# Quantised adapter FFN: h and g transposed as pairs of bytes, scale rows through DRAM, new orders on every engine

## The chip, the cores and the metric

One core of a Trainium2 chip runs the kernel. The metric is device time in microseconds (us). The kernel before has a median of 359.89 us over 3 runs, from 357.31 to 361.01.

## The reference

For each of the 8 batches b, x[b] is 256 tokens by 1024 features, in float32.

- The adapter product: y = x[b] @ W[ids[b]]^T, where W has 16 adapters of 1024x1024 and ids picks one for each batch.
- The FFN on y: a layer norm with gamma and beta gives h. Then two "dynamic quant" linears with an exact GELU between them:

```
s  = max(|row|) / 127                  (one scale for each row, of activations and of weights)
q  = clip(round(row / s), -127, 127)   (whole numbers from -127 to 127)
f1 = (q_h @ q_w1^T) * s_h * s_w1 + b1
g  = gelu(f1)
f2 = (q_g @ q_w3^T) * s_g * s_w3 + b3
out = x + f2
```

## The kernel before

**Tiling.** A batch has two token tiles t of 128 rows. PSUM holds a_ps (two banks, the adapter product), f_ps (two banks, everything of the FFN) and t_ps (four banks, transposed adapter weights).

**The adapter product** is made exact enough by splitting x and W into a high and a low part in a rounded float32 format: three matmuls hi*hi, hi*lo, lo*hi (L1114 to L1116, `products`). A batch has four units u, each of two pieces k. One piece is 12 matmuls of 128x512 on PE (`piece`, L1119). W comes from DRAM in units of 1 MB into the two buffers of w_nat. DVE transposes it in 32x32 blocks into t_ps (`transpose_w`), ACT rounds the high part (`split_w`), DVE subtracts to get the low part (`low_w`). x goes the same way, its low part on POOL (`low_x`).

**The FFN of batch f** runs inside the turn p = f + 1 of a loop over batches. The stages for each token tile:

1. ACT normalises y, POOL multiplies by gamma and adds beta (`scale_and_shift`), DVE takes the row maximum and the scale (`scales_h`), and ACT scales and rounds (`round_h`, by adding the constant 1.5*2^23, so that the whole number stands in the low 16 bits of the float32 word).
2. PE transposes those 16-bit halves (`transpose_h`, `transpose_tile` L1141), eight 128x128 blocks a tile, the tiles into one bank of f_ps each. ACT copies them as int16 to bf16 (`take_h`).
3. PE multiplies by w_q[0] (`ffn1`, 16 matmuls of 128x512 a tile), DVE rescales (`rescale1` L901), POOL adds b1, ACT does GELU, DVE takes the maximum (`scales_g`), ACT rounds (`round_g`).
4. The same again for g: `transpose_g`, `take_g`, `ffn2`, then `scale_ffn2` on ACT, and on POOL the weight scales, the residual and b3 (`finish`, `residual`).

**The head** treats batches 0 and 1: their x and W are transposed on PE (`transpose_first`, 20 steps in FIRST), and the 16 row tiles of w1 and w3 are scaled, rounded, transposed and taken (`max_prep`, `round_prep`, `prepare`, `take_prep`). The two rows of weight scales are made on PE and ACT:

```
for i in range(RT):
    column = wq_scale[:, RT * n + i:RT * n + i + 1].broadcast_to([P, P])
    dst = f_ps[:, i // RB, (i % RB) * P:(i % RB + 1) * P]
    last = pe.transpose(dst, column, ident[:])
```

**The loop** is turns p = 2 to 6. **The tail** (`last_period` on PE, ACT and DVE) finishes batch 7 and the FFNs of batches 6 and 7, with a_ps and t_ps as further banks for the FFN.

**What sets the order.** Each engine has its own in-order list, written out by hand; semaphores tie them. All loads and stores are issued from the SP queue, also in order: a wait of one blocks all behind it. PE's order of a turn before:

```
piece(p, 2, 0)   transpose_h(p - 1, 0), (p - 1, 1)   piece(p, 2, 1)   ffn1(p - 1, 0)
piece(p, 3, 0)   piece(p, 3, 1)                      ffn1(p - 1, 1)
piece(p + 1, 0, 0)  transpose_g(p - 1, 0)            piece(p + 1, 0, 1)  ffn2(p - 1, 0)
piece(p + 1, 1, 0)  transpose_g(p - 1, 1)            piece(p + 1, 1, 1)  ffn2(p - 1, 1)
```

## Time and profile before

| | |
|---|---|
| median of 3 runs | 359.89 us |
| the profiled execution | 362.2 us, span 360.4 us, granted clock 0.99 |
| PE busy | 338.1 us (94%) |
| DVE busy | 282.6 us (78%) |
| POOL busy | 264.3 us (73%) |
| ACT busy | 226.4 us (63%) |
| DMA | 67.35 MB, 70.2% of 16 engines' span |

PE is the matmul side of TensorE, PEld its weight loads. A matmul's duration in the rows contains the overlap with its neighbours: the distance of one start to the next tells what one costs. "Idle before" names who released an engine that stood still. The span runs from the first to the last instruction of the core.

### The profile page before, as it was taken

What the parts mean: (1) busy time and instruction counts of PE and PEld (TensorE: products, weight loads), DVE (VectorE), ACT (ScalarE), POOL (GpSimd) and SP (SyncE); (2) the same over time, 40 slices, a digit from 0 to 9 for tenths busy, and PEclk for the clock granted to TensorE, in tenths of its full rate; (3) what the DMA queues carried; (4) which work ended last, traced back from release to release, by engine and by line L of the source; (5) the groups of instructions that cost most, each with busy time, mean ns of one, the idle gap of its engine ahead of it and who ended that gap; (6) DMA issues with size and microseconds to landing.
All of it is one profiled execution on the core that took longest, in us unless ns stands there. A gap on an engine that the chain in (4) does not pass through costs nothing. (4 is left out here: it accounts for less than half of the span.)

```text
span 360.4 us, 5778 instructions
## 1 busy us (share of the span) xinstructions
PE 338.1 (94%) x1854; PEld 234.1 (65%) x1880; DVE 282.6 (78%) x344; ACT 226.4 (63%) x232; POOL 264.3 (73%) x164
## 2 busy tenths in 40 slices
PE   5899999998887999999899999999999999999885
PEld 5788888865753666676665666566666666665442
DVE  0669888879676589798779878788879877979866
ACT  2443668856976567874596468756777478525640
POOL 1503279545997799976999689978997899956840
PEclk9999999999998999999999999999999999999989
DMA  7999986791995399479962999099946990150014
GB/s 240 362 391 411 400 241 122 182 222 56 241 220 128 103 240 215 86 197 260 221 137 87 301 223 202 3 259 260 217 79 166 295 239 0 59 176 1 0 57 177
DMA packets 46203, 67.35 MB, mean 187 GB/s; under 512 B 2918, under 2 KB 37734, under 8 KB 46186
## 3 DMA queue, kind: packets, MB, share of 16 engines
q1 hardware_dynamic: 46186, 67.14, 70.2%
q8 instruction: 9, 0.15, 0.2%
q14 instruction: 8, 0.07, 0.1%
HBM read 58.74 MB, written 8.39 MB: 186 GB/s over the span
## 5 line engine op out<-in xcount | busy, mean ns | idle before, releaser
L1114 PE MATMUL a_ps<-w_hi,x_hi 128*128 128x512 f32 x256 | 106.6, 416 | 1.8 <-ACT y L608 1.7
L1116 PE MATMUL a_ps<-w_hi,x_lo 128*128 128x512 f32 x256 | 100.1, 391 | 0.0
L1115 PE MATMUL a_ps<-w_lo,x_hi 128*128 128x512 f32 x256 | 99.8, 390 | 0.0
L1168 PE MATMUL f_ps<-w_q,q_t 128*128 128x512 bf16 x377 | 89.8, 385 | 3.7 <-ACT q_t L646 2.5
L593 ACT ACTIVATE w_hi<-t_ps 128x1024 fp32r<-128x1024 f32 x48 | 48.3, 1020 | 39.2 <-DVE t_ps L828 39.0
L1168 PEld LDWEIGHTS f_ps<-w_q,q_t 128*128 128x128 bf16 x400 | 37.6, 99 | 51.1 <-issue 7.5
L828 DVE STREAM_TRANSPOSE t_ps<-w_nat 128x1024 f32<-128x1024 f32 x48 | 58.0, 1240 | 14.5 <-DMA w_nat<-in_L_cond_weight 14.4
L834 DVE TENSOR_TENSOR w_lo<-t_ps,w_hi 128x1024 fp32r<-128x1024 f32 x48 | 57.2, 1215 | 4.5 <-ACT w_hi L593 4.3
L1114 PEld LDWEIGHTS a_ps<-w_hi,x_hi 128*128 128x128 f32 x256 | 48.2, 188 | 14.0 <-ACT y L608 3.1
L1116 PEld LDWEIGHTS a_ps<-w_hi,x_lo 128*128 128x128 f32 x256 | 48.0, 188 | 10.6
L1115 PEld LDWEIGHTS a_ps<-w_lo,x_hi 128*128 128x128 f32 x256 | 48.3, 189 | 9.0
L487 POOL TENSOR_TENSOR a<-a,rows 128x1024 f32<-128x1024 f32 x14 | 33.6, 2398 | 12.3 <-DVE a L901 10.0
L492 POOL TENSOR_TENSOR x_lo<-x_t,x_hi 128x1024 fp32r<-128x1024 f32 x12 | 28.6, 2379 | 14.1 <-ACT x_hi L599 14.1
L483 POOL TENSOR_TENSOR x_res<-x_res,rows 128x1024 f32<-128x1024 f32 x14 | 33.4, 2408 | 4.7 <-DMA x_res<-in_x 4.7
L475 POOL TENSOR_TENSOR o<-o,w_scale_row 128x1024 f32<-128x1024 f32 x12 | 29.4, 2454 | 4.3 <-ACT o L651 4.3
L478 POOL TENSOR_TENSOR o<-o,x_res 128x1024 f32<-128x1024 f32 x12 | 29.6, 2466 | 0.9
L469 POOL TENSOR_TENSOR y<-y,rows 128x1024 f32<-128x1024 f32 x12 | 28.6, 2386 | 0.9
L467 POOL TENSOR_TENSOR y<-y,rows 128x1024 f32<-128x1024 f32 x12 | 28.6, 2387 | 0.0
L869 DVE TENSOR_REDUCE h_max<-y 128x1 f32<-128x1024 f32 x14 | 16.8, 1203 | 10.6 <-POOL y L469 10.6
L901 DVE SCALAR_TENSOR_TENSOR a<-f_ps,h_scale,w_scale_row 128x512 f32<-128x512 f32 x24 | 17.2, 739 | 7.8 <-PE f_ps L1168 7.8
L877 DVE TENSOR_REDUCE g_max<-a 128x1 f32<-128x1024 f32 x14 | 17.0, 1215 | 7.1 <-ACT a L637 6.5
L819 DVE TENSOR_TENSOR w_lo<-t_ps,w_hi 128x1024 fp32r<-128x1024 f32 x14 | 16.9, 1217 | 6.8 <-ACT w_hi L588 6.8
(151 smaller groups left out, 492.1 us busy)
## 6 DMA issues: line engine op xcount, KB each, us to landing
w_nat<-in_L_cond_weight SPq DMA_DIRECT2D x96, 256.0 KB, 6.7
x_res<-in_x SPq DMA_DIRECT2D x7, 1024.0 KB, 7.0
out<-o SPq DMA_DIRECT2D x14, 512.0 KB, 3.0
x_nat<-in_x SPq DMA_DIRECT2D x24, 256.0 KB, 9.6
w_nat<-in_L_cond_weight SPq DMA_DIRECT2D x10, 512.0 KB, 7.2
w_q<-in_L_ffn_w SPq DMA_DIRECT2D x4, 512.0 KB, 10.2
h_r<-in_L_cond_weight SPq DMA_DIRECT2D x4, 512.0 KB, 8.1
w_scale_row<-in_L_ffn_w SPq DMA_DIRECT2D x3, 512.0 KB, 13.3
```

The source lines that it names most:

```text
L467: pool.tensor_tensor(row, row, gamma_row, ALU.mult).then_inc(gamma_done, 1)
L475: pool.tensor_tensor(o[:, t, :], o[:, t, :], w_scale_row[:, 1, :], ALU.mult).then_inc(out_scaled, 1)
L478: pool.tensor_tensor(o[:, t, :], o[:, t, :], x_res[:, t, :], ALU.add).then_inc(out_ready, 1)
L483: pool.tensor_tensor(x_res[:, t, :], x_res[:, t, :], b3_row, ALU.add).then_inc(x_b3_ready, 1)
L487: pool.tensor_tensor(a[:, t, :], a[:, t, :], b1_row, ALU.add).then_inc(ffn1_biased, 1)
L593: act.activation(part_of_unit(w_hi, u, k), piece_bank(k), ACT.Copy).then_inc(w_hi_ready, 1)
L828: dve.transpose(piece_bank(k).rearrange("p c (kb s) -> p kb c s", s=BLK), w_nat[:, u % 2].rearrange("p kb (c r) -> p kb c r", r=BLK)[:, :, ...
L834: dve.tensor_tensor(part_of_unit(w_lo, u, k), piece_bank(k), part_of_unit(w_hi, u, k).bitcast(F32), ALU.subtract).then_inc(w_lo_ready, 1)
L1114: pe.matmul(ps, hi, w_hi[:, u, c], start=begin, stop=False)
L1115: pe.matmul(ps, hi, w_lo[:, u, c], start=False, stop=False)
L1116: last = pe.matmul(ps, lo, w_hi[:, u, c], start=False, stop=end)
L1168: last = pe.matmul(ps[:, half, :], q[:, c, :], w[:, c, half_of(half)], start=c == 0, stop=c == CB - 1)
```

## The change

1. `round_h` and `round_g` write int8 (no constant added) into parts of the tile h_r. PE transposes pairs of bytes as one 16-bit word: four blocks a tile where there were eight. Both h tiles go to bank 0 of f_ps. `take_h` and `take_g` read bytes from PSUM at a step of two and write the same bf16 tiles. The weights are transposed with 16-bit elements at a step of four (before: two), so that their order fits.
2. The scale rows: a DMA stores the column of scales to DRAM, another loads them as a row broadcast to 128 partitions. The 16 transposes and two ACT copies go.
3. Tail: four tensor_tensor additions on DVE's list become scalar_tensor_tensor with a multiplication by 1.0; two small POOL operations go for each tile; the last half product is cut in two quarters of 256 columns, each with its own scaling, addition and store; orders are new.
4. Orders of the head, the loop and the tail are new on every engine; the first unit starts with its hi*hi products before the low part is there. All FFN work of head and loop stays in f_ps.

```
-                act.activation(h_r[:, t, :], rows_of(f)[:, t, :], ACT.Identity, scale=h_inv[:, t:t + 1], bias=magic[:]
-                               ).then_inc(h_rounded, 1)
+                act.activation(h_8[t], rows_of(f)[:, t, :], ACT.Identity, scale=h_inv[:, t:t + 1]).then_inc(h_rounded, 1)
...
+        def words_of(bank, t=0):
+            return bank[:, WORDS * t:WORDS * (t + 1)].bitcast(BF16).rearrange("p (c k) -> p c k", k=P)
...
+        def bytes_in(bank, tiles=1):
+            return bank[:, 0:WORDS * tiles].bitcast(I8).rearrange("p (c k b) -> p c b k", k=P, b=PACK)
...
             def take_h(f):
-                act.activation(q_t[:].rearrange("p t c k -> p (t c k)"),
-                               f_ps[:].bitcast(I16).rearrange("p h n -> p (h n)"), ACT.Copy).then_inc(h_t_ready, 1)
+                act.activation(blocks_in(q_t[:].rearrange("p t c k -> p (t c) k")), bytes_in(f_ps[:, 0], TT), ACT.Copy
+                               ).then_inc(h_t_ready, 1)
...
-            def transpose_tile(src, bank, done):
-                halves = src.bitcast(BF16).rearrange("p (k two) -> p k two", two=2)[:, :, 0]
-                blocks = transposed(bank, BF16)
+            def transpose_tile(src, blocks, done):
+                words = src.bitcast(BF16)
+                for c in range(CB // PACK):
+                    last = pe.transpose(blocks[:, c, :], words[:, c * P:(c + 1) * P], ident_16[:])
+                last.then_inc(done, 1)
+
+            def transpose_weights(src, blocks, done):
+                halves = src.bitcast(BF16).rearrange("p (c k b two) -> p c b k two", k=P, b=PACK, two=2)
                 for c in range(CB):
-                    last = pe.transpose(blocks[:, c, :], halves[:, c * P:(c + 1) * P], ident_16[:])
+                    last = pe.transpose(blocks[:, c, :], halves[:, c // PACK, c % PACK, :, 0], ident_16[:])
...
+            def store_scales(n):
+                sp.wait_ge(wq_scale_ready, len(PARTS) // 2 * (n + 1))
+                sp.dma_start(scale_scratch[n].rearrange("(i p) -> p i", p=P), wq_scale[:, RT * n:RT * (n + 1)],
+                             allow_slow_non_contiguous=True
+                             ).then_inc(scales_stored[n], 16)
+            def load_scale_row(n):
+                sp.wait_ge(scales_stored[n], 16)
+                sp.wait_ge(wq_transposed, (RT, 14)[n])
+                sp.dma_start(w_scale_row[:, n, :], scale_scratch[n:n + 1, :].broadcast_to([P, D])
+                             ).then_inc(scale_row_loaded[n], 16)
...
                 for t in range(TT):
+                    if ch == 0 and k == 0:
+                        wait_past(pe, y_copied, UNITS * b + TT * (kh - 1) + t + 1)
                     last = products(u, t, k, a_ps[:, t, :])
...
             def period(p):          # PE
-                piece(p, 2, 0)
                 transpose_h(p - 1, 0)
                 transpose_h(p - 1, 1)
+                piece(p, 2, 0)
+                ffn1(p - 1, 0)
                 piece(p, 2, 1)
-                ffn1(p - 1, 0)
+                ffn1(p - 1, 1)
                 piece(p, 3, 0)
                 piece(p, 3, 1)
-                ffn1(p - 1, 1)
+                transpose_g(p - 1, 0)
                 piece(p + 1, 0, 0)
-                transpose_g(p - 1, 0)
+                ffn2(p - 1, 0)
                 piece(p + 1, 0, 1)
-                ffn2(p - 1, 0)
+                transpose_g(p - 1, 1)
                 piece(p + 1, 1, 0)
-                transpose_g(p - 1, 1)
+                ffn2(p - 1, 1)
                 piece(p + 1, 1, 1)
-                ffn2(p - 1, 1)
...
             def period(p):          # POOL
+                add_b1(p - 1, 0)
                 low_x(p + 1, 0)
-                add_b1(p - 1, 0)
+                add_b1(p - 1, 1)
                 residual(p - 1)
+                normalisers_of(p)
                 low_x(p + 1, 1)
-                normalisers_of(p)
-                add_b1(p - 1, 1)
                 scale_and_shift(p, 0)
                 scale_and_shift(p, 1)
                 finish(p - 1, 0)
...
             def period(p):          # DVE
+                transpose_x(p + 1)
                 transpose_w(p + 1, 0, 0)
+                rescale1(p - 1, 0)
                 transpose_w(p + 1, 0, 1)
-                transpose_x(p + 1)
                 low_w(p + 1, 0, 0)
+                transpose_w(p + 1, 1, 0)
+                rescale1(p - 1, 1)
+                scales_g(p - 1, 0, a[:, 0, :], 0)
                 low_w(p + 1, 0, 1)
-                rescale1(p - 1, 0)
-                transpose_w(p + 1, 1, 0)
-                transpose_w(p + 1, 1, 1)
                 low_w(p + 1, 1, 0)
-                scales_g(p - 1, 0, a[:, 0, :], 0)
                 statistics(p, 1)
                 mean_and_variance(p)
+                transpose_w(p + 1, 1, 1)
                 transpose_w(p + 1, 2, 0)
...
                 transpose_w(p + 1, 3, 0)
+                scales_h(p, 0, 0)
                 transpose_w(p + 1, 3, 1)
-                scales_h(p, 0, 0)
                 scales_h(p, 1, 1)
...
             ffn1(0, 0)              # PE, the head
-            piece(1, 3, 1)
             ffn1(0, 1)
...
             transpose_g(0, 0)
             ffn2(0, 0)
+            piece(2, 1, 0)
             transpose_g(0, 1)
             ffn2(0, 1)
+            piece(2, 1, 1)
...
             # ACT, the tail: take_g of tile (6, 1), before behind both halves of the last GELU
                 gelu(f, 0)
                 round_h_last(1)
...
+                gelu_last()
+                take_g_before(1)
+                gelu_half(0)
+                round_g_last(0)
+                gelu_half(1)
+                take_g_last(0)
...
-                    dve.tensor_tensor(part, part, b1_row[:, half_of(half)], ALU.add).then_inc(last_half_biased, 1)
+                    dve.scalar_tensor_tensor(part, part, 1.0, b1_row[:, half_of(half)], ALU.mult, ALU.add
+                                             ).then_inc(last_half_biased, 1)
...
+                def ffn2_last_quarter(n):
+                    for c in range(CB):
+                        last = pe.matmul(last_quarter(n), q_last[:, 1, 1, c, :],
+                                         w_q[1][:, c, D - BANK // 2 * (2 - n):D - BANK // 2 * (1 - n)],
+                                         start=c == 0, stop=c == CB - 1)
```

## Rows read from the trace of the kernel before

**Rows 1.** Windows, all engines: PE busy, PEld, DVE, ACT, POOL busy, clock, DMA share, GB/s.
```profile
0.00:115.89 115.89, 104.70 (x678) 82.01 (x681) 84.03 (x98) 71.66 (x76) 65.23 (x57) 0.99 0.84 246
115.89:309.34 193.45, 189.28 (x943) 126.94 (x961) 158.75 (x193) 133.10 (x135) 170.50 (x90) 1.00 0.75 179
309.34:360.40 51.06, 44.09 (x237) 25.19 (x240) 39.80 (x55) 21.60 (x22) 28.57 (x18) 0.96 0.22 83
```

**Rows 2.** Windows, the same columns: one turn of the loop.
```profile
235.81:274.45 38.64, 37.87 (x189) 25.36 (x193) 32.23 (x40) 26.66 (x28) 34.33 (x19) 1.00 0.83 190
```

**Rows 3.** Timeline of PE in that turn: start, us, engine, line, operands, [idle before].
```profile
235.81 1.07 PE L1145 MATMUL f_ps<-ident,h_r 128*128 128x128 bf16 x16
236.69 0.48 PE L1114 MATMUL a_ps<-w_hi,x_hi 128*128 128x512 f32 x1
...
255.10 0.48 PE L1114 MATMUL a_ps<-w_hi,x_hi 128*128 128x512 f32 x1
...
257.94 3.63 PE L1168 MATMUL f_ps<-w_q,q_t 128*128 128x512 bf16 x15
...
271.59 0.50 PE L1114 MATMUL a_ps<-w_hi,x_hi 128*128 128x512 f32 x1 [0.55 <-ACT y L608]
```

**Rows 4.** Timeline of PE in the head: scale row, waits before and in ffn2(0).
```profile
64.79 1.03 PE L1241 MATMUL f_ps<-ident,wq_scale 128*128 128x128 f32 x8
...
104.51 3.40 PE L1168 MATMUL f_ps<-w_q,q_t 128*128 128x512 bf16 x15 [1.34 <-ACT q_t L646]
...
110.93 5.31 PE L1168 MATMUL f_ps<-w_q,q_t 128*128 128x512 bf16 x16 [1.12 <-ACT q_t L646]
```

**Rows 5.** Chain of waits of the whole run, in the same turn: start, us, what.
```profile
251.94 2.41 POOL x_lo L492
...
255.59 2.42 POOL a L487
...
265.25 2.41 POOL y L469
...
267.69 1.23 DVE h_max L869
```

**Rows 6.** Timeline of ACT, end of that turn.
```profile
269.33 1.24 ACT L620 ACTIVATE h_r<-y,magic,h_inv 128x1024 f32<-128x1024 f32 x1 [1.53 <-DVE h_inv L865]
...
275.56 1.88 ACT L632 ACTIVATE q_t<-f_ps 128x2048 bf16<-128x2048 int16 x1 [0.48 <-PE f_ps L1145]
```

**Rows 7.** DMA issues of the page: count, KB each, median us to landing.
```profile
w_nat<-in_L_cond_weight SPq DMA_DIRECT2D x96, 256.0 KB, 6.7
...
w_scale_row<-in_L_ffn_w SPq DMA_DIRECT2D x3, 512.0 KB, 13.3
```

**Rows 8.** Timeline of PE in the tail.
```profile
343.34 3.48 PE L1168 MATMUL t_ps<-w_q,q_t 128*128 128x512 bf16 x8 [2.68 <-ACT q_t L706]
...
352.72 3.62 PE L1168 MATMUL f_ps<-w_q,w_nat 128*128 128x512 bf16 x16
```

**Rows 9.** Timeline of ACT in the tail.
```profile
342.28 1.00 ACT L706 ACTIVATE q_t<-t_ps 128x1024 bf16<-128x1024 int16 x1
```

**Rows 10.** Timeline of DVE in the tail.
```profile
317.79 1.31 DVE L953 SCALAR_TENSOR_TENSOR y<-y,mean_var,rows 128x1024 f32<-128x1024 f32 x1
...
339.64 2.06 DVE L983 TENSOR_TENSOR w_nat<-w_nat,rows 128x512 f32<-128x512 f32 x1
...
356.38 0.75 DVE L1028 SCALAR_TENSOR_TENSOR x_t<-f_ps,g_scale,w_scale_row 128x512 f32<-128x512 f32 x1 [0.18 <-PE f_ps L1168]
357.16 0.69 DVE L1032 TENSOR_TENSOR x_t<-x_t,x_nat 128x512 f32<-128x512 f32 x1
```

**Rows 11.** Timeline of POOL in the tail.
```profile
317.97 1.17 POOL L451 TENSOR_TENSOR minus_mean<-mean_var,minus_one 128x1 f32<-128x1 f32 x1
...
336.05 5.11 POOL L483 TENSOR_TENSOR x_res<-x_res,rows 128x1024 f32<-128x1024 f32 x2
346.38 2.36 POOL L575 TENSOR_TENSOR o<-o,x_res 128x1024 f32<-128x1024 f32 x1 [5.23 <-DVE o L972]
```

More of the change, by code:

```diff
@@ L130, in adaln_ffn_kernel @@
         x_rows = {0: o, 13: x_last}
+        bytes_of = [h_r[:, t, :].bitcast(I8) for t in range(TT)]
+        h_8 = [row[:, 0:D] for row in bytes_of]
+        g_8 = [row[:, D:2 * D] for row in bytes_of]
+        g_8_last = [row[:, 2 * D:3 * D] for row in bytes_of]
+        scale_scratch = nc.dram_tensor("scale_scratch", (2, D), F32, kind="Internal").ap()
         a_ps = psum("a_ps", [P, TT, BANK])
@@ L408, in _ @@
             load_prep((10,))
+            load_unit(2, 1)
             load_x(2)
-            load_unit(2, 1)
             load_unit(2, 0)
+            load_scale_row(0)
+            load_x(3)
             load_prep((15,))
             load_prep((14,))
-            load_unit(2, 2)
             load_prep((13,))
             load_residual(0)
+            load_unit(2, 2)
             load_unit(2, 3)
-            load_x(3)
+            store_scales(1)
+            load_scale_row(1)
             load_unit(3, 0)
@@ L575, in _ @@
                 pool.tensor_tensor(o[:, t, :], o[:, t, :], x_res[:, t, :], ALU.add).then_inc(out_ready, 1)
+            normalisers_last(0)
+            normalisers_last(1)
+            add_b1(f, 0)
+            add_b1(f, 1)
+            add_b1_last()
+            residual(f)
+            finish_before(0)
+            finish_before(1)
         @block.scalar
@@ L705, in take, with gelu_last, gelu_half, round_g_last @@
                     act.wait_ge(ready, n)
-                    act.activation(blocks, transposed(bank, I16), ACT.Copy).then_inc(done, 1)
+                    act.activation(blocks_in(blocks), bytes_in(bank), ACT.Copy).then_inc(done, 1)
+                def gelu_last():
+                    act.wait_ge(ffn1_biased, TT * LAST + 1)
+                    act.activation(a_last[:, 0], a_last[:, 0], ACT.Gelu).then_inc(g_ready, 1)
+                def gelu_half(half):
+                    part = a_last[:, 1, half_of(half)]
+                    act.wait_ge(last_half_biased, half + 1)
+                    act.activation(part, part, ACT.Gelu).then_inc(last_half_gelu, 1)
+                def round_g_last(t):
+                    act.wait_ge(g_inv_ready, TT * LAST + t + 1)
+                    act.activation(g_8_last[t], a_last[:, t], ACT.Identity, scale=g_inv[:, TT + t:TT + t + 1]
+                                   ).then_inc(g_rounded, 1)
+                def take_h_last(t):
+                    take(h_transposed, TT * LAST + t + 1, a_ps[:, t], q_last[:, 0, t], h_t_ready)
+                def take_g_before(t):
+                    take(g_transposed, TT * f + t + 1, (a_ps[:, 0], t_ps[:, 0, 0])[t], q_t[:, t], g_t_ready)
+                def take_g_last(t):
+                    take(g_transposed, TT * LAST + t + 1, (t_ps[:, 1, 0], f_ps[:, 0])[t], q_last[:, 1, t], g_t_ready)
                 take_h(f)
@@ L1117, in products, with first_unit_piece @@
                 return last
+            def first_unit_piece(k):
+                pe.wait_ge(first_hi_ready, first_piece(1, k) + 1)
+                for t in range(TT):
+                    tokens = slice(t * P, (t + 1) * P)
+                    for c in range(CP * k, CP * (k + 1)):
+                        pe.matmul(a_ps[:, t, :], x_hi[:, c, tokens], w_hi[:, 0, c], start=c == 0, stop=False)
+                pe.wait_ge(first_lo_ready, first_piece(1, k) + 1)
+                for t in range(TT):
+                    tokens = slice(t * P, (t + 1) * P)
+                    for c in range(CP * k, CP * (k + 1)):
+                        pe.matmul(a_ps[:, t, :], x_hi[:, c, tokens], w_lo[:, 0, c], start=False, stop=False)
+                        last = pe.matmul(a_ps[:, t, :], x_lo[:, c, tokens], w_hi[:, 0, c], start=False, stop=False)
+                if k == 1:
+                    last.then_inc(w_used, 1)
             def piece(b, u, k):
                 kh, ch = divmod(u, CH)
+                if isinstance(b, int) and b == 0 and u == 0:
+                    first_unit_piece(k)
+                    return
                 if isinstance(b, int) and b == 0:
@@ L1273, in unit, with ffn1_before, transpose_h_last @@
                         last.then_inc(y_done, 1)
-                unit(2, 0)
+                def ffn1_before(half):
+                    pe.wait_ge(h_t_ready, f + 1)
+                    product_half(q_t[:, 1], w_q[0], t_ps[:, 0], half, ffn1_done)
+                def transpose_h_last(t):
+                    pe.wait_ge(h_rounded, TT * LAST + t + 1)
+                    pe.wait_ge(y_copied, UNITS * LAST + TT + t + 1)
+                    transpose_tile(h_8[t], words_of(a_ps[:, t]), h_transposed)
@@ new lines, in ffn2_before, with transpose_g_last @@
+                def ffn2_before(t, half):
+                    pe.wait_ge(g_t_ready, TT * f + t + 1)
+                    if t == 0 and half == 1:
+                        pe.wait_ge(h_t_ready, LAST + 2)
+                    if t == 1:
+                        pe.wait_ge(ffn1_scaled, KH * (TT * f + 1) + half + 1)
+                    product_half(q_t[:, t], w_q[1], (a_ps, t_ps[:, 0])[t], half, ffn2_done)
+                def transpose_g_last(t):
+                    pe.wait_ge(g_rounded, TT * LAST + t + 1)
+                    if t == 0:
+                        pe.wait_ge(ffn1_scaled, KH * TT * LAST + 1)
+                    else:
+                        pe.wait_ge(last_half_scaled, 1)
+                    transpose_tile(g_8_last[t], words_of((t_ps[:, 1, 0], f_ps[:, 0])[t]), g_transposed)
```

476 lines of the change are left out of this document (240 added, 236 removed).

## The prediction

> **What bounds the kernel now.** I read the windows first. In the loop PE is busy 189.3 of 193.45 us, in the head 104.7 of 115.9, in the tail 44.1 of 51.1 [rows 1]. In a turn of 38.64 us the others have room by their sums: DVE 32.2, POOL 34.3, ACT 26.7, DMA 83% of the time [rows 2]. So the loop goes by PE's own work, and what leaves PE's list counts until another chain takes over. The timeline of PE shows what a turn is made of: both h tiles' 16 transposes take 0.88 us (235.81 to 236.69), a piece of adapter product 2.8 (255.10 to 257.94), a product of FFN about 3.5, and one wait of 0.55 us for ACT's copy of y [rows 3]. In the head PE stood still 11.2 us. Of that, 2.5 lies at ffn2(0), whose second product also took 5.31 us [rows 4], where the one in rows 3 takes 3.63. In the tail it waits 2.68 us for ACT's q_t, and then eight matmuls take 3.48 us [rows 8], where 16 take 3.62 at the end: half the pace, 1.2 in place of 2.4 GHz.
>
> **The profiled execution** took 362.2 us (span 360.4), the median of the runs is 359.9. I make the sum against 360.4 and take the same difference off the median.
>
> **Part 1, transposes of byte pairs.** A block costs 0.88 / 16 = 0.055 us [rows 3]. Of 256 blocks (8 batches, 32 each) 128 go: 7.0 us of PE time. In the head these are 16 (0.9 us), in each of 5 turns 16 (0.9), and the rest lie in the tail. The weights' 128 blocks are read at a step of 8 bytes, before 4. No row shows that step: at no cost it is 0, at double time 7 us in the head. I take 0, since a step of 4 bytes runs no slower than the rate that 128 columns at 2.4 GHz give (0.053). ACT's copies read bytes at a step of two. The nearest rows are 1.88 us for two tiles of int16 [rows 6] and 1.00 for one [rows 9]: I take the same, since elements are as many; the other end is double. Rounding without the constant: 1.24 us [rows 6] or less.
>
> **Part 2, scale rows.** Two groups of eight float32 transposes of 1.03 us each leave PE [rows 4]: 1.9 us without the overlap. Two ACT copies go, beside other work. New are a store of 1024 single elements and a load of 512 KB for each row, on SP's queue. The nearest loads land in 13.3 us [rows 7]. Row 0 is wanted at rescale1(0, 0); by my walk below it is issued at about 62 and wanted at 70. With the DMA queue less full than early on I take 6.7 us [rows 7], so no wait; at 13.3 it is 5 us, once. What the store itself takes has no row: 2 to 5 us, an estimate from the smallest loads of rows 7, and SP stands at load_scale_row until it landed; load_x(3) and later load_unit(3, 0) are behind it, both wanted more than 8 us later.
>
> **Part 3, the order of the loop.** I walked one turn with the durations of the rows, from the start of transpose_h = 0. PE: piece(2,0) at 0.5, ffn1(0) at 3.3, piece at 6.7, ffn1(1) 9.5 to 12.9, two pieces to 18.4, transpose_g, piece, ffn2(0) at 21.4, piece, transpose_g, piece, ffn2(1) at 30.7, piece(1,1) to 36.9. That is PE's floor: 38.64 less 0.9 for transposes and less about 0.8 for the wait of [rows 3] (0.55, and what the modelled end of the matmul before hides), as the transposes of h now stand in front of that piece and its first half asks for one tile of y alone. The other side is the chain that prepares the next h, and the chain of waits shows its steps [rows 5]: x_lo 2.41, the four normaliser operations 1.2 (254.35 to 255.59), additions and products of POOL 2.4 each, h_max and scale to the round 1.65 (267.69 to 269.33), the round 1.24 [rows 6]. ffn1(1) ends at 12.9, rescale to 13.9; then on POOL without a gap add_b1(1), residual (two), normalisers, low_x, four of scale_and_shift: 13.9 + 8 x 2.4 + 1.2 + 0.1 = 34.4, then 1.7 + 1.2 = 37.3, and 0.3 for handing over: **37.6 us**. Before, transpose_h came 2.7 us later, behind a piece, and this chain had slack; now it binds by 0.7. So a turn goes from 38.7 (193.45 / 5) to 37.6: **5.5 us over five**. What else I checked in the walk: take_h is done at 3.1 against 3.3 (ACT copies y first, and that is the least slack), take_g twice with 1 us, the first rescale at 5.9 behind DVE's transpose_x, finish ends 1.1 us before add_b1 of the next turn. SP: the load of unit 3 waits for transpose_w(1,1), which now stands behind the statistics, and is issued at 21.9; with 6.7 us and 1.9 of issuing it is there at 29 to 30.5, as DVE wants it at 29.2. No stall, but no slack.
>
> **Part 4, the head.** Transposes 0.9, scale row 1.9. Between ffn2(0,0) and transpose_g(0,1) there is now a piece: the wait of 1.3 for ACT's eviction goes, and the clock should stay up, 5.31 - 3.63 = 1.7. The waits of 1.34 and 1.12 for q_t stay [rows 4], since transpose_g and ffn2 are still neighbours. ffn1(0,1) now follows ffn1(0,0) with nothing between: +1.0, a latency of 0.25 and one rescale of 0.75 [rows 10]. The start: x half 1 is loaded before unit 0, all four pieces of data are there when they were before, and piece(0,0,0) begins about 13.8 where one transpose began at 13.3: +0.5 at worst, with hi*hi ahead of the low part covering DVE. POOL's normalisers and h(0) come some 3 us earlier, and need to, as transpose_h(0) is two pieces earlier: even. Sum **4.8 us**.
>
> **Part 5, the tail.** take_g of tile (6,1) is no longer behind both GELU halves, so the 2.68 of wait and the slow clock (3.48 - 1.8 = 1.7) go. Against it: round_h_last(1) is now behind gelu(6,0), +0.9 before its transpose; g of (7,1) still needs DVE's addition, which is late because of POOL. DVE's addition took 2.06 where 0.69 is its time alone [rows 10], as POOL's residual ran until 341.16 [rows 11]: each waits for the other to end. Is scalar_tensor_tensor free of this? POOL's product of one element a row took 1.17 us, until 319.14, and DVE's scalar_tensor_tensor on y ran until 319.10 [rows 10, 11]. So I take it to hold POOL up, and to be held up, just so: gain 0. At the end DVE then has two scalings for tile 0 of batch 6, two for tile 1, and five scale-and-add pairs of about 0.75 + 0.7 (two of them quarters, 0.9 each), with two waits of some 1.5 for POOL's additions of 2.36 [rows 11]. From the last scale at 344.6 this gives an end of DVE at 355.5, before 357.85; PE is through at 351.7. With the last store, **2.4 us**. If scalar_tensor_tensor is free of POOL it is 4.2.
>
> The Trainium skill, Vector Engine (DVE) Microarchitecture Reference, section Points that are easy to get wrong, says that this instruction with two non-bf16 SBUF sources runs at half throughput. By that rule the four additions of this change would cost some 0.6 us more each and the tail's gain would be gone. The row on y disagrees: 1024 elements took 1.31 us, as much as one element a cycle.
>
> **Sum.** 4.8 + 5.5 + 2.4 = 12.7: span 347.7, profiled about 349.5, median **347.2 us**.
>
> **Rivals.**
>
> - *PE never gets its time back in the loop* (chance 0.21). The h chain or the y copy is a microsecond later than walked and a turn stays at 38.7. For: I find only 0.2 us of slack at take_h, and POOL, at 34.3 of 38.6 us, is nearly full. Against: its steps are short and regular in the rows. Then 4.8 + 2.4: 352.7.
> - *The loop reaches PE's floor* (0.10). 36.9 a turn: the constant gone from round_h and handing over shorter than taken. 9.0 + 4.8 + 2.4 to 4.2: 341.9 to 343.7.
> - *Slower: the reload of unit 3* (0.07). The place is DVE's transpose_w(3,0), ahead of scales_h of both tiles. Landing takes 6.7 us in the median, but it is 13.3 for loads in crowded stretches [rows 7]. Each us later than 1.5 past the median delays transpose_h by one, five times. It decides at 40.1 a turn (landing 11 us after the issue): from there on nothing is won. At 13.3 a turn is 42.2: 359.9 - 7.2 + 17.5 = 370. Against: DMA is busy 83% of the turn as before, and residual and x are through by then.
> - *Bytes cost double on ACT, or the weights' step on PE* (0.08). take_h 1.88 us longer of which 0.2 is covered, five turns (8), three copies in the head (4): 359. The weights alone, 7 in the head: 354.
> - *The scale row comes late* (0.04): 5 us, 352.
>
> **How the numbers follow.** The forecast has 0.50. The likeliest's own range: 344 to 350, from the tail's 4.2 and the two transfers. To hold 8 in 10 the whole range needs the first two rivals: from 342.5 to 354.5. A measurement of this kernel tells 1% (3.6 us) from nothing, since its runs spread by that. Faster by more than 1% (below 356.3) are the forecast, the first two rivals, the late row and half of the byte rival: 0.88. Within 1%: half of the byte rival and a little of the reload: 0.06. Slower: 0.06.
>
> **What would show it.** PE: transposes of h x8 in 0.45 us, no 0.55 wait before piece(p,2,0). The loop's turn 37.6, with PE idle 0.5 to 0.7 before transpose_h, released by ACT's round_h: if it is idle elsewhere (ffn1 behind take_h, say) the walk failed there. ACT's take_h 1.88 and take_g 1.00 again. Weights' transposes 0.055 apart. No wait of rescale1(0,0) for the DMA. In the tail no wait of 2.68, and the additions on DVE still 1.4 to 2.1 us where POOL runs. I am wrong if a turn is above 38.3, or if the additions take 0.75 beside POOL.

## The result: 357.0 us, about a quarter of the forecast gain

The changed kernel has a median of 357.03 us over 20 runs (353.81 to 359.03), the one before 360.54 over 20 runs. The ratio is 0.9915, with a 95% interval from 0.9888 to 0.9943: some 3 us won where 12.7 were forecast, and outside the range given. The profiled execution of the changed kernel has a span of 355.7 us. Medians are over all runs of a kernel; the ratios leave out the runs that were over 1.5% slower than the fastest of the same kernel, such as the profiled one of the kernel with the loads ahead below.

The page of the changed kernel, its line of engines, the bandwidth in 40 slices and the packets; behind them the packets of the kernel before:

```profile
PE 333.7 (94%) x1744; PEld 230.7 (65%) x1744; DVE 284.5 (80%) x346; ACT 220.4 (62%) x230; POOL 264.2 (74%) x160
...
GB/s 252 351 377 374 349 156 248 165 241 158 231 121 100 239 251 222 192 68 297 210 217 42 293 227 213 84 217 281 207 121 152 299 103 155 62 177 1 2 0 236
DMA packets 48714, 68.39 MB, mean 192 GB/s; under 512 B 5046, under 2 KB 40118, under 8 KB 48698
```

```profile
DMA packets 46203, 67.35 MB, mean 187 GB/s; under 512 B 2918, under 2 KB 37734, under 8 KB 46186
```

The 2128 more packets of under 512 bytes are, but for some 80, the elements of the two stores. PE's busy time fell by 4.4 us, the span by 4.7. The same three stretches as [rows 1]. The head now ends with the first transpose of h in the loop, which opens the turn (before, the turn opened with a piece and h came behind it):

```profile
0.00:116.60 116.60, 104.52 (x648) 83.53 (x648) 80.19 (x94) 69.17 (x74) 61.84 (x56) 0.97 0.87 240
116.60:304.60 188.00, 186.38 (x881) 122.87 (x880) 161.74 (x195) 130.38 (x134) 172.98 (x92) 1.00 0.81 192
304.60:355.70 51.10, 42.77 (x217) 24.27 (x216) 42.55 (x58) 20.81 (x23) 29.34 (x14) 0.94 0.23 83
```

Columns: stretch and its length, then busy time of PE, weight loads, DVE, ACT and POOL, the granted clock, the DMA share and GB/s. The loop took 188.0 us, five turns of 37.6: to the tenth what was forecast. The head took 116.6 where 111.1 was forecast (it was 115.9), the tail 51.1 where 48.7 was (it was 51.1). So the whole miss of the profiled execution is 5.5 us in the head and 2.4 in the tail.

**The head.** PE's timeline at the place where it stood still longest (start, duration, operation, and in brackets the idle time before it and who ended it):

```profile
63.14 1.94 PE L1322 MATMUL t_ps<-ident,w_nat 128*128 128x128 f32 x8 [4.32 <-DVE w_lo L889]
64.87 1.06 PE L1260 MATMUL f_ps<-ident,w_scale_row 128*128 128x128 bf16 x8
65.72 1.15 PE L1322 MATMUL t_ps<-ident,w_nat 128*128 128x128 f32 x8
```

After 4.32 us of waiting the first group takes 1.94 us, the third, of the same shape, 1.15: the clock had fallen from its upper level. Why was the low part late? DVE's timeline just before:

```profile
54.74 1.22 DVE L956 TENSOR_REDUCE wq_max<-x_res 128x1 f32<-128x1024 f32 x1 [2.37 <-DMA x_res<-in_L_ffn_w]
58.39 1.22 DVE L956 TENSOR_REDUCE wq_max<-x_res 128x1 f32<-128x1024 f32 x1 [2.42 <-DMA x_res<-in_L_ffn_w]
59.52 2.34 DVE L956 TENSOR_REDUCE wq_max<-o 128x1 f32<-128x1024 f32 x2
61.77 2.35 DVE L889 TENSOR_TENSOR w_lo<-t_ps,w_hi 128x1024 fp32r<-128x1024 f32 x2
```

The low parts stand in DVE's list behind the maxima of weight tiles 9 to 12, and two of these waited 4.8 us in all for their loads. SP's queue issued them here:

```profile
39.17 3.39 SPq L366 DMA_DIRECT2D w_nat<-in_L_cond_weight  x2
42.61 0.43 SPq L386 DMA_DIRECT2D scale_scratch<-wq_scale  x1
43.08 0.87 SPq L381 DMA_DIRECT2D x_res<-in_L_ffn_w  x1
44.00 0.43 SPq L381 DMA_DIRECT2D o<-in_L_ffn_w  x1
44.48 0.44 SPq L381 DMA_DIRECT2D x_res<-in_L_ffn_w  x1
```

Two suspects stand side by side. The loads moved behind the last rows of W, which wait for a buffer until 42.2; in the kernel before they were issued from 38.75 to 40.9. And right in front of them stands the new store of 1024 single scales (L386). The second load was waited for until 58.4, 13.9 us after its issue.

**The tail.** The 2.68 of [rows 8] is gone, and a wait of the same size is there for something else:

```profile
328.41 0.40 PE L1254 MATMUL a_ps<-ident,h_r 128*128 128x128 bf16 x4 [2.86 <-ACT h_r L689]
328.64 3.49 PE L1283 MATMUL t_ps<-w_q,w_nat 128*128 128x512 bf16 x8
```

```profile
326.26 1.06 ACT L699 ACTIVATE a<-a 128x1024 f32<-128x1024 f32 x1 [3.10 <-POOL a L538]
327.22 1.13 ACT L689 ACTIVATE h_r<-y,h_inv 128x1024 int8<-128x1024 f32 x1
```

ACT's list has gelu(6, 0) ahead of the round of h(7, 1). The GELU waits for POOL's addition (322.90 to 326.23), and the round, whose input was ready about 325.7, waits with it. Behind the wait eight matmuls take 3.49 us at the lower clock, again as in [rows 8].

### The profile page after: what moved, and what is told of

Same layout as the page of the kernel before. It is cut to its first block, busy times and chain, and to the rows that moved or that the text cites. A ratio compares the mean times of both kernels' runs of the same rounds, so it can differ in the third digit from the quotient of the medians.

```text
span 355.7 us, 5548 instructions
## 1 busy us (share of the span) xinstructions
PE 333.7 (94%) x1744; PEld 230.7 (65%) x1744; DVE 284.5 (80%) x346; ACT 220.4 (62%) x230; POOL 264.2 (74%) x160
## 4 chain that ended last, share of the span: by engine, by line
PE 57%; DVE 13%; DMA 11%; POOL 8%; issue 5%; ACT 4%; SPq 2%; DVEq 0%; ACTq 0%; POOLq 0%
PE f_ps L1283 17%; PE a_ps L1205 11%; PE a_ps L1207 10%; PE a_ps L1206 10%; DMA w_nat<-in_L_cond_weight 6%; DMA x_res<-in_L_ffn_w 4%; POOL a L538 2%; DVE x_nat L1019 2%; PE t_ps L1335 2%; PE f_ps L1260 2%; DVE t_ps L898 1%; DVE h_max L939 1%; POOL y L520 1%; POOL x_lo L543 1%; POOL y L518 1%
## 5 line engine op out<-in xcount | busy, mean ns | idle before, releaser
L1205 PE MATMUL a_ps<-w_hi,x_hi 128*128 128x512 f32 x248 | 103.9, 419 | 0.5 <-ACT y L672 0.2
L1207 PE MATMUL a_ps<-w_hi,x_lo 128*128 128x512 f32 x248 | 97.0, 391 | 0.0
L1206 PE MATMUL a_ps<-w_lo,x_hi 128*128 128x512 f32 x248 | 96.6, 390 | 0.0
L898 DVE STREAM_TRANSPOSE t_ps<-w_nat 128x1024 f32<-128x1024 f32 x48 | 59.3, 1244 | 9.6 <-DMA w_nat<-in_L_cond_weight 8.5
L657 ACT ACTIVATE w_hi<-t_ps 128x1024 fp32r<-128x1024 f32 x48 | 48.3, 1019 | 23.8 <-DVE t_ps L898 23.5
L1205 PEld LDWEIGHTS a_ps<-w_hi,x_hi 128*128 128x128 f32 x248 | 46.6, 188 | 12.0 <-ACT y L672 1.0
L1207 PEld LDWEIGHTS a_ps<-w_hi,x_lo 128*128 128x128 f32 x248 | 46.5, 188 | 10.4
L1206 PEld LDWEIGHTS a_ps<-w_lo,x_hi 128*128 128x128 f32 x248 | 46.7, 188 | 8.8
L652 ACT ACTIVATE w_hi<-t_ps 128x1024 fp32r<-128x1024 f32 x14 | 13.9, 1025 | 16.2 <-PE t_ps L1322 8.2
L921 DVE BATCH_NORM_STATS2 stats<-y 128x6 f32<-128x512 f32 x26 | 17.5, 689 | 7.6 <-ACT y L672 7.5
```

What stands on the lines that cost most here:

```text
L657: act.activation(part_of_unit(w_hi, u, k), piece_bank(k), ACT.Copy).then_inc(w_hi_ready, 1)
L898: dve.transpose(piece_bank(k).rearrange("p c (kb s) -> p kb c s", s=BLK), w_nat[:, u % 2].rearrange("p kb (c r) -> p kb c r", r=BLK)[:, :, ...
L1205: pe.matmul(ps, hi, w_hi[:, u, c], start=begin, stop=False)
L1206: pe.matmul(ps, hi, w_lo[:, u, c], start=False, stop=False)
L1207: last = pe.matmul(ps, lo, w_hi[:, u, c], start=False, stop=end)
```

## The experiments

All ratios are to the kernel before, on the same chip as the experiment, with 95% intervals. "Changed kernel" is the one of the diff; an edit is against it unless another is named. Heads and loops are measured by the same marks as above.

### The byte pairs alone, in the old order

The kernel before with nothing but part 1 of the change:

```
-  last = pe.transpose(... 16-bit halves, 8 blocks a tile)
+  last = pe.transpose(... byte pairs, 4 blocks a tile)     # and take_*, round_* to match
```

> The kernel before with the byte pairs alone: int8 rounds, four transposed blocks a tile in place of eight, byte copies, the weights' step of four; all orders, the scale rows and the tail as before. Theory: the transposes were plain PE time, a turn goes from 38.64 to 37.8 us and keeps its wait of 0.55 for y, the copies of ACT cost the same; over the kernel some 7 us less (128 blocks of 0.055). Rival: other chains (POOL, the loads) hold a turn at over 38.3, and the gain is under 3 us.

Measured: 358.5 us, ratio 0.9888 (0.9821 to 0.9955), span 356.9: between the two expectations, some 4 us less by the ratio. It is no worse than the whole change at 0.9915, so the other parts together won nothing that these runs show. The loop took 192.1 us from one first h to the other (118.13 to 310.25), against 193.4 before. PE's list is 0.9 us a turn shorter, 4.5 in all, and 3.2 of them came back: a turn is 38.4, as the rival had it. PE's waits in that stretch (total us, times, longest), in the kernel before and in this one:

```profile
PE a_ps L1114 <- ACT y L608: 1.7, 3, 0.6
PE f_ps L1145 <- DVE a L901: 1.4, 2, 1.0
```

```profile
PE a_ps L1140 <- ACT y L635: 2.7, 5, 0.7
PE f_ps L1170 <- DVE a L927: 2.4, 3, 1.2
```

3.1 us of recorded waits became 5.1. In the new order neither of the two is recorded in the loop. So the shorter transposes need the order with h at the front of the turn as well; what that order would win without them was not run.

The tail of this kernel, in the old order, took 49.5 us from the first piece of its turn (307.44 to 356.90), against 51.06 before. Its wait is longer than the 2.68 of [rows 8], but the clock stayed up behind it:

```profile
341.88 1.90 PE L1199 MATMUL t_ps<-w_q,q_t 128*128 128x512 bf16 x7 [3.21 <-ACT q_t L732]
```

### The order of loads, of DVE's list and of the start

Four kernels take the head's order apart. The first two load the maxima's tiles before the last rows of W and the store, the second of them with the start undone as well:

```
+  load_prep((9,)) ; load_prep((12,)) ; load_prep((10,))
   load_rows_of_w((7,))
   store_scales(0)
-  load_prep((9,)) ; load_prep((12,)) ; load_prep((10,))
```

> The changed kernel with the loads of weight tiles 9, 12, 10 issued ahead of the adapter rows 7 and of the scale store. Theory: in the head DVE's maxima of tiles 9 and 10 wait 2.4 us twice for these loads, low_first(16) stands behind them, and PE waits 4.32 us for it and then runs slow; issued some 4 us earlier, the tiles are there, PE's wait is under 0.5, and the loop begins at about 111.5 instead of 116.6. Rival: the DMA engines are full up to 60 us, so that the tiles land no earlier than before or another load comes late in their place; then the loop begins at 114 or later.

Measured: 352.91 us, 0.9699 (0.9620 to 0.9778). In the profiled execution (355.3 us) the loop began at 114.4 in place of 116.6. The wait of 4.3 was gone, but 2.9 us of it came back at 76.7, where rescale1(0, 0) was late.

```
   load_first_unit(0)
+  load_first_x((1,))            # was ahead of unit 0
...
+  transpose_first(4)
   piece(0, 0, 0)                # was ahead of transpose_first(4)
```

> As the kernel with the loads ahead, and the start undone as well: x half 1 is loaded behind unit 0 and transpose_first(4) stands ahead of the first piece. Theory: the 1.4 us of wait before the second transpose step and the half clock behind it (0.78 granted from 9.7 to 17.4 us) go, and transpose_first(5) starts at 17.0 in place of 18.3: 1.3 us less at the start, and as much at the loop's begin if DVE and DMA keep up. Rival: what is won at the start is waited for again before 70 us, since loads set the pace there; the loop begins within 0.4 us of the kernel with the loads ahead alone.

Measured: 350.69 us, 0.9684 (0.9614 to 0.9754); the loop began at 110.6.

The start alone undone:

> The changed kernel with only the start as it was: x half 1 loaded behind unit 0, the first transpose of unit 4 ahead of the first product. Theory A (what PE loses at the start is kept to the end of the head): the wait of 1.4 us at 9.7 and the slow clock after it go, PE reaches transposes of unit 5 about 1.3 us earlier, and the first transposes of h in the loop come at about 115.3 in place of 116.6; median 1.3 us lower. Theory B (the head goes by the arrival of the preps' rows of x, at 58 us, whatever PE does before): the wait for w_lo at 63 grows by what the start wins, 4.3 to 5.5 us, and the first transposes of h come at 116.6 again; time unchanged.

Measured: 357.47 us, 0.9909 (0.9866 to 0.9953). The wait at 63 was 5.54 us and the loop began at 117.9. What the start wins is lost at the load that comes at its own time. So the 1.3 us that PE lost at the start of the changed kernel cost nothing so long as the load was late.

DVE's low parts ahead of the maxima, the loads left as they were:

```
+  low_first(16) ; low_first(17)
   max_prep((9, 10, 11, 12))
-  low_first(16) ; low_first(17)
```

> The changed kernel with one edit in DVE's order: the low parts of units 16 and 17 ahead of the maxima of tiles 9 to 12, with the loads where the change put them. Theory A (PE waits 4.3 us at 63 only because DVE stands in line behind two late loads of maxima): the wait for w_lo at 63 goes, the maxima end as late as before, and the head is 3 to 4 us shorter unless PE then waits at the first h or at transpose_x for what stands behind the maxima; then the wait comes back there with 2 to 4 us and the head is the same. Theory B (DVE is full there, and the wait is its sum): the wait moves to the next low part and stays about 4 us.

Measured: 353.35 us, 0.9801 (0.9727 to 0.9874). The loop began at 113.7. The wait at 63 shrank to 0.56, and 3.31 us came at 76.2, again for rescale1. Each of these edits leaves a wait or brings a new one: there is a row of transfers that land late, and whoever is ordered behind the next of them waits.

### The tail: the round ahead of the GELU

```
   take_h_last(0)
+  round_h_last(1)
   gelu(f, 0)
-  round_h_last(1)
```

> The changed kernel with one swap in ACT's tail: round of h tile (7,1) ahead of GELU of tile (6,0). Theory: ACT's in-order list holds the round back, since the GELU waits for POOL's add_b1, which took 3.33 us beside DVE's scalar_tensor_tensor. Then PE's wait of 2.86 us before the last h transposes shrinks to about 1.5 and the eight matmuls behind it take 1.7 in place of 3.49 us; the tail, 51.07 us from the last turn's transposes of h (304.63) to the end, becomes about 48. Rival: the wait only moves to the transposes of g, or the end is set by DVE and POOL alone; then the tail stays within 1 us of 51.

Measured: 356.77 us, 0.9815 (0.9749 to 0.9882). Tail 49.1 in place of 51.1; ACT's round now starts as its input is there:

```profile
327.97 1.15 ACT L689 ACTIVATE h_r<-y,h_inv 128x1024 int8<-128x1024 f32 x1 [2.53 <-DVE h_inv L935]
329.03 1.04 ACT L699 ACTIVATE a<-a 128x1024 f32<-128x1024 f32 x1
```

PE's wait is 1.34 and the clock stays up. In this run the head lost more than before (a wait of 7.6 us for w_lo, start of the loop at 119.6), so the median shows little of it: the head varies with its transfers. The ratio is 1% under that of the changed kernel; four runs on another chip do not tell how much of that is the tail.

All three orders together (start, loads, tail):

> The changed kernel with three orders put right together: x half 1 loaded behind unit 0 and the first transpose of unit 4 ahead of the first product (as before the change), the loads of tiles 9, 12 and 10 for the maxima ahead of the loads of the last rows of w and of the scale store, and in the tail ACT's round of tile (7,1) ahead of the GELU of tile (6,0). Theory (the head's loss is load order, the tail's is ACT's order, and they add): first transposes of h in the loop at 110.5, loop 186.4 to 188, tail 49: span 346 to 347.5, median about 349 on this chip, 1.5 to 2 us below the version without the tail's edit. Rival (the tail ends by DVE's own row of sums, so that an earlier round buys nothing there): tail 50.9 again, median 350.7.

Measured: 348.86 us, 0.9638 (0.9568 to 0.9708), span 348.2, tail 49.0. The tail's gain adds. But the loop began at 112.7, where the kernel with the same head above began it at 110.6: there were 3.06 us of waiting for rescale1. SP's queue shows something that no order explains:

```profile
45.59 4.49 SPq L312 DMA_DIRECT2D w_nat<-in_L_cond_weight  x4
50.13 7.80 SPq L323 DMA_DIRECT2D x_nat<-in_x  x4
...
69.08 1.80 SPq L323 DMA_DIRECT2D x_nat<-in_x  x4
```

Four issues of the same kind took 7.80 us at 50 and 1.80 at 69. Something held the queue after the store.

### The tail's sums as tensor_tensor again

```
-  dve.scalar_tensor_tensor(part, part, 1.0, ..., ALU.mult, ALU.add)
+  dve.tensor_tensor(part, part, ..., ALU.add)              # four places
```

> The changed kernel with the tail's additions on DVE as tensor_tensor again, all four places, nothing else. Theory A (scalar_tensor_tensor with two SBUF operands shares POOL's port just as tensor_tensor does): the tail stays at 51.1, DVE's additions beside POOL's keep 1.5 to 2.0 us, POOL's product of one element a row keeps 1.4, its additions 5.1 for two; time unchanged within 0.5 us. Theory B (the form matters, and one of the two lets POOL through): durations of POOL's rows beside these additions move by more than 0.5 us each, the two additions on x_last from 6.6 to 4.5 us as in the kernel before, and the tail moves by 1 us or more.

Measured: 357.6 us, 0.9940 (0.9894 to 0.9986). The additions to x_last, in the changed kernel and in this one:

```profile
307.10 6.58 DVE L1019 SCALAR_TENSOR_TENSOR x_nat<-x_nat,rows 128x1024 f32<-128x1024 f32 x2
```

```profile
307.24 6.58 DVE L1019 TENSOR_TENSOR x_nat<-x_nat,rows 128x1024 f32<-128x1024 f32 x2
```

6.58 us for both forms, beside the same POOL operations (2.39 and 3.26 us each time). The tail took 49.63 us, while two profiles of kernels with scalar_tensor_tensor, in which the clock also stayed up behind the wait of 2.9, took 49.66 (the low parts ahead, above) and 49.67 (the store in runs, below). The edit of the sums is worth nothing that these runs show, and the tail's 1.5 us against 51.1 are the clock.

### The store of the scales

One line: each partition's eight scales go out as one run of 32 bytes, 128 runs in place of 1024 single elements. The scale rows then hold the values in a wrong order; the work is the same otherwise, and start, loads and tail stay as the change has them.

```
-  sp.dma_start(scale_scratch[n].rearrange("(i p) -> p i", p=P), wq_scale[...])
+  sp.dma_start(scale_scratch[n].rearrange("(p i) -> p i", p=P), wq_scale[...])
```

> The changed kernel, but both stores of the scales write each partition's eight scales as one run of 32 bytes: 128 runs in place of 1024 single elements. The scale rows then hold the right values in a wrong order; all else is the same work. Theory A (the 1024 single elements hold the DMA queue, so that the rows of w for the maxima land 13.9 us after their issue and DVE and PE wait): the store lands in 3 to 6 us instead of 10 to 15, tile 10 lands some 4 us earlier, at about 54, PE's wait of 4.3 us at 63 shrinks to under 1, the head is about 4 us shorter, median near 353.5. Theory B (the queue is full there with the loads themselves, and the maxima's rows are late because they were issued 4 us later than in the kernel before): tile 10 still lands at 57 to 58, PE waits 3.5 to 5.5 us at 63, the head and the median move by less than 1 us.

Measured: 348.37 us, 0.9679 (0.9608 to 0.9750): 5 us less than this experiment expected, and near the 347.2 of the prediction. The stretches:

```profile
0.00:109.40 109.40, 101.14 (x646) 80.38 (x648) 82.23 (x94) 69.23 (x74) 63.25 (x56) 1.00 0.85 263
109.40:295.90 186.50, 185.11 (x866) 122.83 (x880) 161.41 (x195) 130.47 (x135) 171.87 (x91) 1.00 0.79 190
295.90:345.60 49.70, 40.93 (x214) 23.84 (x216) 43.45 (x58) 21.02 (x23) 29.35 (x14) 0.96 0.23 85
```

The head is 7.2 us shorter, the loop 1.5, the tail 1.4. Not all of this is the store's. The tail's part is the clock: the wait of 2.85 is still there, but the seven matmuls recorded behind it take 1.89 us. Loops of kernels that keep the single elements took from 186.3 (the start undone) to 188.6 us (the low parts ahead), so the loop's part is not shown to be the store's. And 1.6 us of the head were there before the store was issued, at 40.98 in this kernel and at 42.61 in the changed one. The same transposes at the start, first in the changed kernel, then here:

```profile
11.18 1.86 PE L1335 MATMUL f_ps<-ident,w_nat 128*128 128x128 f32 x8 [0.41 <-DMA w_nat<-in_L_cond_weight]
```

```profile
11.22 1.09 PE L1335 MATMUL f_ps<-ident,w_nat 128*128 128x128 f32 x8 [0.41 <-DMA w_nat<-in_L_cond_weight]
```

The granted clock from 9.7 to 17.4 us was 0.78 there and 1.00 here, in the same order of work. From the store's issue to the loop took 74.0 us in the changed kernel and 68.4 here. Two more kernels have the head of the changed kernel unaltered, and took longer: 76.0 (the sums undone) and 78.7 (the round ahead). So the store costs this head 5.6 us or more.

The DMA view from 40 to 62 us shows why. First the changed kernel: the busy share of the DMA engines in tenths and the bandwidth, both in 40 slices of 0.55 us, packets by size, and the median from issue to landing:

```profile
DMA  9889999999999991539399962899899999999999
GB/s 294 287 290 331 395 421 421 439 402 417 293 182 300 209 89 7 30 37 104 82 119 127 104 52 60 298 328 328 346 300 251 210 218 209 244 229 210 210 246 229
DMA packets 3700, 5.14 MB, mean 234 GB/s; under 512 B 1235, under 2 KB 2518, under 8 KB 3700
...
x_res<-in_L_ffn_w SPq DMA_DIRECT2D x2, 512.0 KB, 12.8
```

Then the one with runs of 32 bytes:

```profile
GB/s 346 376 421 421 428 384 426 390 434 335 425 373 477 357 333 236 296 233 169 188 205 203 229 214 222 238 225 216 222 237 209 158 153 91 35 22 0 22 168 356
DMA packets 3722, 5.76 MB, mean 262 GB/s; under 512 B 394, under 2 KB 2735, under 8 KB 3721
x_res<-in_L_ffn_w SPq DMA_DIRECT2D x2, 512.0 KB, 8.3
...
scale_scratch<-wq_scale SPq DMA_DIRECT2D x1, 4.0 KB, 5.9
```

For some 6 us, from 47.7 to 53.7, the core moved 7 to 127 GB/s in the changed kernel, and 169 to 333 in this one: with means of 74 and 230 that is 0.9 MB less in 6 us, beside 4 KB of scales. The elements themselves come just before: 1076 of the 1371 packets from 44 to 48 us are under 512 bytes, and from 48 to 54 there are 138 packets in all, while the loads issued before 45 have not landed. Why the loads' packets are held there no view tells. The loads for the maxima, issued behind the store in both kernels, land in 8.3 us in place of 12.8. DVE's waits for them shrink from 4.8 to 0.6:

```profile
50.66 1.21 DVE L956 TENSOR_REDUCE wq_max<-x_res 128x1 f32<-128x1024 f32 x1
52.48 1.22 DVE L956 TENSOR_REDUCE wq_max<-x_res 128x1 f32<-128x1024 f32 x1 [0.61 <-DMA x_res<-in_L_ffn_w]
```

The same edit where the three orders were already put right:

> The same edit of the store (128 runs of 32 bytes, scales in a wrong order) on the version with the three orders put right, which still waits 3.1 us for rescale1 of batch 0 at 75.7. Theory A (the single elements' store is behind that wait, since x_nat, w_nat and the scale row land late behind it): issuing x_nat at 50 takes 2 to 3 us instead of 7.8, the wait falls under 1.3 us, the head is 2 to 3 us shorter: median 346 to 347. Theory B (DMA is full from 54 on with data alone): the wait stays 1.7 to 3.1, median 348.5 to 349.5.

Measured: 346.78 us, 0.9633 (0.9563 to 0.9703), span 344.2. The wait for rescale1 went from 3.06 to 0.85, issuing x_nat from 7.80 to 2.64. From 48 to 57 us the core moved 97 GB/s on average with the single elements and 213 with the runs: the hole, and its end, a second time. In time the gain is small here: the ratios are 0.9638 and 0.9633, but the runs with the single elements spread from 346.4 to 355.3 us and these from 346.0 to 347.6. The order of the loads and of the start, which had looked like 6 us, is worth 0.6 once the store is in runs (the loop begins at 108.8 instead of 109.4); the tail's edit keeps its 0.6. The two repairs of the head stand in for each other: either of them alone takes most of the loss away, the order to 110.6 and 112.7, the store to 109.4.

### A version that keeps the scales in order

```
+  dve.transpose(wq_scale_t[n][:], wq_scale[:])             # 128x32, in 32x32 blocks
+  for b in range(P // BLK):
+      first = b * BLK + n * RT
+      sp.dma_start(scale_scratch[n].rearrange("(i b s) -> b i s", i=RT, s=BLK)[b],
+                   wq_scale_t[n][first:first + RT, :]).then_inc(scales_stored[n], 16)
```

> The version with the three orders put right, and the scales stored in their right order by a cheap way: DVE turns the 128x32 tile of scales in 32x32 blocks, and four stores of 8 runs of 128 bytes follow. Costs: DVE 0.1 to 0.2 us twice, three more issues on SP of 0.43 us each row. If the single elements' store is what crowds the queue: the four land in 3 to 6 us, and the time is that of the version with 32-byte runs, 346 to 347. If not: 349, as without it.

Measured: **346.20 us** (346.03 to 347.0), 0.9615 (0.9564 to 0.9665), span 344.3: faster than both kernels, and 10.8 us below the changed one by their medians, or 0.9615 against 0.9915 as ratios. The four stores took SP 1.36 us to issue. Its packets:

```profile
DMA packets 46762, 68.39 MB, mean 199 GB/s; under 512 B 3094, under 2 KB 38166, under 8 KB 46746
```

With DVE's low parts ahead as well:

> The version before this one with DVE's low parts of units 16 and 17 ahead of the maxima of tiles 9 to 12 as well. If DVE still stands in line behind a late load of a maximum: 0.5 to 1 us less than the version before. If those loads are in time (they were, once they are issued ahead of the other rows): the same within 0.5 us, or up to 1 us more where the scales of h(0), now 2.3 us later behind nothing new, set POOL's and ACT's work on w_q back.

Measured: 347.18 us (346.86 to 347.64), 0.9640 (0.9589 to 0.9690), the loop from 109.7 instead of 109.0. What won 3 us while the loads were late costs 0.7 to 1 once they are not.

## Why the prediction was wrong, step by step

- **Scale rows (part 2) and the head (part 4): the step that failed.** The prediction gave the store 2 to 5 us of landing, though the smallest load of [rows 7] takes 6.7, and asked only whom SP's standing would delay. What the store does to transfers behind it in the queue it put at nothing without a reason, and part 4 had no term for the loads of the maxima, which the change moves behind the store and the last rows of W. The store landed in 10.7 us (the second; for the first the profile of the changed kernel has no landing, and five others have 11.1 to 15.8). That SP stood was not the point. The loads behind it were: landing 12.8 us where the same loads in the same place take 8.3, with a hole of 6 us in the bandwidth. The one line that makes runs of the elements shows it: from the store's issue to the loop 68.4 us in place of 74.0 to 78.7, and a head of 109.4, 1.7 better than the 111.1 forecast. The loss needs the order too: with the loads ahead of the store and the start undone the head was 110.6 and 112.7.
- **The rival "the scale row comes late"** had the right object and the wrong victim. Rescale1 did wait for the row itself in some kernels (0.5 to 1.0 us), but first came the waits of DVE for data that has nothing to do with scales.
- **The start**: a loss of "0.5 at worst" was 1.3 (transpose 5 at 18.27 against 16.98): PE waits 1.41 for W until 9.7, and the clock falls to 0.78. That was this execution: in the kernel with runs PE waits 1.51 at the same place in the same order, the clock stays up, and transpose 5 starts at 16.67. The loss did not reach the end while the load at 58 ruled, and is at most 0.6 without it.
- **The other waits of the head**: forecast 1.34 and 1.12 for q_t and 1.0 for ffn1(0, 1); measured 1.11, 1.12 and 0.85. The 1.7 of slow clock at ffn2(0) did not recur.
- **The loop**: 37.6 forecast and measured, but by two errors that met. PE's floor is 37.3, not 36.9: with the store in runs a turn takes (295.9 - 109.4) / 5 = 37.3, with no wait of PE recorded in the loop, and just so with the single elements in the kernel with the start undone (186.3 / 5). And the chain that was to bind by 0.7 us a turn hardly does: transpose_h waits for ACT's round in two turns of the changed kernel (0.9 us together) and in neither of those two kernels. That the sum came out to the tenth is luck. The turn's start shows where the floor was put too low:

```profile
267.31 0.71 PE L1254 MATMUL f_ps<-ident,h_r 128*128 128x128 bf16 x8
268.11 0.50 PE L1205 MATMUL a_ps<-w_hi,x_hi 128*128 128x512 f32 x1
...
270.96 3.63 PE L1283 MATMUL f_ps<-w_q,q_t 128*128 128x512 bf16 x16
```

  Eight blocks take 0.80 us to the next start, where 16 took 0.88 in [rows 3] and eight would take 0.44. The 0.36 between is most likely the rest of the wait for y, which I had let vanish. So the rival "the loop reaches PE's floor" was right in its mechanism and 0.4 us a turn too low in its size. The rival of the late reload did not come; its own terms give 42.7 us a turn at 13.3, not 42.2.
- **Bytes and the weights' step cost nothing extra**: take_h 1.88 and take_g 1.01 us as in [rows 6, 9], the round 1.15 against 1.24, weights' transposes 219 to 223 ns each where the clock was up, as those of h at 221. That rival fell.
- **The tail**: 2.4 us were forecast and none came. "Round_h_last(1) behind gelu(6, 0)" was put at 0.9, with the clock up. PE's wait there is 2.86, because the GELU stands behind an addition of POOL that takes 3.3; with that one line turned 1.34 are left, so the order cost 1.5 at that place and 0.6 at the end (49.65 against 49.05). On top the clock fell for 1.4 us in some profiles (tail 51.1) and not in others (49.65). The last 0.4 to the forecast is a wait of 0.5 us at g(7, 1), which only the kernels with that line turned show. And what the prediction took back from [rows 8] was in part the clock too: with the byte pairs alone, the old order and the clock up, the tail took 49.5. So the new order of the tail is not shown to win anything by itself.
- **scalar_tensor_tensor** holds POOL up, and is held up, like tensor_tensor: as argued, now shown by 6.58 us in either form. Nor is its rate halved: where POOL stands, 512 elements take 0.69 us in either form.

DVE's last additions beside POOL in the changed kernel, for [rows 10, 11]:

```profile
346.37 0.90 DVE L1078 SCALAR_TENSOR_TENSOR x_t<-x_t,x_nat 128x512 f32<-128x512 f32 x1
...
348.04 1.98 DVE L1078 SCALAR_TENSOR_TENSOR x_t<-x_t,x_nat 128x512 f32<-128x512 f32 x1
...
350.80 0.69 DVE L1078 SCALAR_TENSOR_TENSOR x_t<-x_t,x_nat 128x512 f32<-128x512 f32 x1
```

```profile
344.36 5.11 POOL L630 TENSOR_TENSOR o<-o,x_res 128x1024 f32<-128x1024 f32 x2 [3.92 <-DVE o L1042]
```

The one behind POOL's end (349.47) takes 0.69, the one into it 1.98.

**Open**: whether the store is slow by the number of its elements (1024) or by their size (4 bytes). The runs changed both at once, and no kernel separated them. Nor is it known when the clock falls: behind the same wait of 2.85 us in the tail it fell in some profiles and not in others, and so at the start.

## What to carry to other kernels

Price a transfer by its pieces, not by its bytes, and charge it to everything else in the queue while it is under way: the sign here was a hole in GB/s while loads issued before it had not landed. The share of busy DMA engines did not tell: in those slices it lay anywhere from 1 to 9 tenths. When waits wander from one place to the next as you repair orders, look for one thing upstream of them all before taking any of the repairs for a gain. In an in-order list a ready operation behind one that waits for a third engine stands as long as that one (here 1.5 us of PE's 2.86), and the clock may fall behind it. And before a difference of two profiles is put down to an edit, look whether it is there already ahead of the edited place: 1.6 of 7.2 us were.

## What the runs showed of the hardware

- A store of 1024 single 4-byte elements landed 10.4 to 15.8 us after its issue, beside full traffic; one of 128 runs of 32 bytes in 5.7 to 5.9 in one kernel, in 5.7 and 11.4 in the other. The hole in the bandwidth came only with the single elements.
- Behind it four issues on the same queue took up to 7.80 us, with the runs up to 2.82; later in the kernel they take 1.80.
- ACT reading every second byte from PSUM takes as long as reading 16-bit elements that lie side by side (1.88 us for 128x2048), and PE transposes 16-bit elements at a step of 8 bytes as fast as at 4.
